# A graph network on one core: POOL's rests moved between chunk gathers and node gathers

## The reference

```python
# layer L0 (src, dst of all edges)
h = einsum('ni,hio->nho', x, W_att)
alpha = segment_softmax(leaky_relu(h[src] @ a_src + h[dst] @ a_dst), dst)
local = segment_sum(alpha * h[src], dst).mean(heads)
glob = x
for _ in range(2):                                   # two hops
    glob = segment_sum(glob[src], dst) / deg
x = x + concat(local, glob @ W_g + b_g) @ W_w + b_w
# layers L1, five times
h = leaky(x @ W1 + b1) @ W2 + b2
e = leaky(edge_attr @ We1 + be1) @ We2 + be2
out = x + segment_sum(h[src] * e * dot_scale, dst) * res_w
x = layernorm(out) * ln_g + ln_b
```

## Time and profile before

| | us |
|---|---|
| median of 3 runs | 6910.15 |
| lowest, highest | 6908.07, 6911.17 |
| the profiled execution | 6893.8 |
| its span, first to last instruction | 6892.0 |
| POOL busy in the span | 5142.3 (75%) |
| DVE busy | 5197.8 (75%) |
| PE busy | 5232.0 (76%) |

### The profile page before, as it was taken

How to read it: one execution, slowest core, us unless ns; L and a number is a source line. 1 busy time by engine, 2 the same in 40 slices (tenths; PEclk the granted TensorE clock), 3 DMA queues, 4 the chain that set the end, 5 groups by cost and what they waited for, 6 DMA issues and landing times.

```text
span 6892.0 us, 140780 instructions
## 1 busy us (share of the span) xinstructions
PE 5232.0 (76%) x51990; PEld 4800.9 (70%) x51995; DVE 5197.8 (75%) x12225; ACT 4110.2 (60%) x6886; POOL 5142.3 (75%) x7040
## 2 busy tenths in 40 slices
PE   7888843333333489998799997999979999799997
PEld 6878732222222388888788887888878888788887
DVE  7877666666666578888688886888878888688887
ACT  4666626555555356666466664666646666466664
POOL 6777777777777467776677775777757777577776
PEclk9999965656555689999899997999979999799998
DMA  4444426777777433333233332333323333233332
GB/s 108 109 106 113 107 69 229 240 245 238 240 236 241 139 85 100 99 97 97 66 97 101 98 98 68 98 99 97 98 67 98 99 96 97 68 96 98 97 99 76
DMA packets 505340, 828.89 MB, mean 120 GB/s; under 512 B 110911, under 2 KB 218038, under 8 KB 491599
## 3 DMA queue, kind: packets, MB, share of 16 engines
q1 hardware_dynamic: 373374, 655.05, 28.3%
q0 software_dynamic: 131280, 164.84, 13.4%
HBM read 385.06 MB, written 434.48 MB: 119 GB/s over the span
## 4 chain that ended last, share of the span: by engine, by line
PE 52%; issue 7%; DVE 4%; ACT 1%; another core or an unknown queue 1%; POOL 1%; DMA 0%; POOLq 0%; DVEq 0%; ACTq 0%
PE psum L1372 45%; PE psum L1386 6%; DVE arena L1773 1%; POOL agg L719 1%; DVE by_lane L1836 0%; ACT gring L1010 0%; PE psum L1298 0%; DVE psum L1819 0%; PE psum L1329 0%; ACT gring L1014 0%; DVE xin L1773 0%; ACT run L995 0%; DVE arena L1790 0%; DMA agg<-rowsg,last_i 0%
## 5 line engine op out<-in xcount | busy, mean ns | idle before, releaser
L712 POOL DMA_INDIRECT gring<-tableh,src_i x2525 | 2480.6, 982 | 863.0 <-issue 587.9
L1372 PE MATMUL psum<-penalty,arena 125*128 125x192 bf16 x25755 | 2474.9, 247 | 248.3 <-issue 227.7
L1372 PEld LDWEIGHTS psum<-penalty,arena 125*128 125x128 bf16 x25755 | 2154.3, 98 | 365.0 <-issue 336.4
L1773 DVE TENSOR_SCALAR arena<-dst_f,node_id 125x768 bf16<-125x768 f16 x4301 | 1762.4, 457 | 0.1
L712 POOL DMA_INDIRECT gring<-table,src_i x1364 | 1384.3, 1015 | 441.2 <-issue 317.1
L703 POOL MEMSET diag<- 128x256 f32 x2916 | 1061.1, 364 | 228.8 <-DMA tableh<-arena 116.7
L985 ACT COPY psum<-diag 128x512 f32<-128x512 f32 x505 | 297.5, 590 | 1338.4 <-issue 765.9
L1813 DVE TENSOR_REDUCE gring<-psum 128x192 f32<-128x576 f32 x505 | 381.9, 756 | 765.9 <-remote 421.2
L1149 PE MATMUL psum<-ident,by_lane 128*128 128x128 f32 x202 | 66.2, 431 | 882.2 <-DMA by_lane<-attr_last 754.6
L1149 PEld LDWEIGHTS psum<-ident,by_lane 128*128 128x128 f32 x202 | 29.1, 203 | 941.1 <-issue 941.1
L923 ACT ACTIVATE arena<-gring,es_w 128x65 f32<-128x65 f32 x1616 | 398.3, 335 | 456.4 <-DMA gring<-table,src_i 445.0
(11 more groups left out here) (280 smaller groups left out, 8748.0 us busy)
## 6 DMA issues: line engine op xcount, KB each, us to landing
rows<-arena SPq DMA_DIRECT2D x101, 1296.0 KB
acts<-arena SPq DMA_DIRECT2D x505, 256.0 KB
arena<-acts SPq DMA_DIRECT2D x505, 256.0 KB
rowsg<-run SPq DMA_DIRECT2D x505, 256.0 KB
dst_f<-pe_src SPq DMA_DIRECT2D x557, 93.8 KB
gring<-tableh,src_i POOLq DMA_INDIRECT x2525
rows<-run SPq DMA_DIRECT2D x101, 256.0 KB
gring<-table,src_i POOLq DMA_INDIRECT x1364
```

What stands on the lines that cost most here:

```text
L712: pool.indirect_dma_start(ring[:, s, k, :], None, table, bass.IndirectOffsetOnAxis(ap=src_i[:, c * K + k:c * K + k + 1], axis=0))\
L1372: ins = mm(found(n)[:, m, :], hot_at(n // 2, j)[:, at:at + P], parts[:, j, :, :].rearrange("q a f -> q (a f)"), start=(j == 0), stop=(j == ...
L1773: ins = ts(hot_at(pair, j), src_row[b], node_id[:, j:j + 1], None, ALU.is_equal)
```

## The change

The counting moves into a helper `paced(burst)`: before a gather, if `burst` gathers were issued since the last rest or reset, it rests and begins to count again. `gather_chunk` gets a parameter `burst` (4 unless given) and `gather_nodes` calls `paced()` before each of its 25 gathers, having set the count to zero. The count is also set to zero ahead of the second pass and ahead of each layer. The second pass calls `gather_chunk` with a burst of K = 8.

```diff
+            def paced(burst=BURST):
+
+                if issued[0] == burst:
+                    pause()
+                    issued[0] = 0
+                issued[0] += 1
+
-            def gather_chunk(c, s, table, ring, ready, cols):
+            def gather_chunk(c, s, table, ring, ready, cols, burst=BURST):
                 for k in range(cols):
-                    if issued[0] and issued[0] % BURST == 0:
-                        pause()
-                    issued[0] += 1
+                    paced(burst)
                     pool.indirect_dma_start(ring[:, s, k, :], None, table,
                                             bass.IndirectOffsetOnAxis(ap=src_i[:, c * K + k:c * K + k + 1], axis=0))\
                         .then_inc(ready[s], 16)
 
             def gather_nodes(rows, to, arrived):
 
+                issued[0] = 0
                 for j in range(NJ):
+                    paced()
                     pool.indirect_dma_start(to[:, j, :], None, rows,
                                             bass.IndirectOffsetOnAxis(ap=last_i[:, j:j + 1], axis=0))\
                         .then_inc(arrived[j // GJ], 16)
...
             pool.wait_ge(t2_out, NG * 16)
             settle()
+            issued[0] = 0
             for c in range(CH):
                 if c >= SL:
                     pool.wait_ge(hopcopy, c - SL + 1)
                     pool.wait_ge(msg_steps, (c - SL + 1) * (K - ON_ACT))
                     settle()
-                gather_chunk(c, c % SL, table2, gather2, g2_ready, K)
+                gather_chunk(c, c % SL, table2, gather2, g2_ready, K, K)
...
                 pool.wait_ge(table_out, (l + 1) * (NG * 16))
                 settle()
+                issued[0] = 0
                 for c in range(CH):
```

## The result

| | before | changed |
|---|---|---|
| median | 6909.11 us (6908.05 to 6911.17, 4 runs) | 6797.38 us (6788.06 to 6801.15, 4 runs) |
| profiled execution | 6893.8 us, span 6892.0 | 6788.06 us, span 6786.2 |
| ratio, 95% interval | | 0.9836, 0.9819 to 0.9853 |

What follows compares the result with a forecast made beforehand. PE was taken to bound the layers, POOL's instruction stream the second pass. Removed rests -103.5, contention +6, added rests +18, resets -1 gave -80 us: 6830 us against the median of 6910.15, range 6806 to 6860 us.

Steps and rivals of the forecast that it cites:

- The second pass: Paced by POOL's instruction stream; 102 rests removed give -103.5 us, with the contention term -97.5 us.
- The contention term: Second pass: with shorter chunks more of DVE's work meets gathers and stretches them, giving back 6 us.
- the one of transfers that give half back: Second pass: gathers queue behind row stores and POOL waits for buffers; 6875 us, chance 0.12.
- the one of stretching gathers: Second pass: gathers without a rest between them stretch to 1.43 us; about 7150 us, slower, chance 0.04.
- DVE's waits for gathers near 1.6 us a chunk: Second pass: sign that the forecast is right, from a mean wait of 2.6 us before.
- Cost of the added rests: Node gathers: 3 us after the first pass, 1 after the second, 8 in layers 0 to 3, 6.2 in layer 4.
- ACT's 8.39 us: Layers 0 to 3, behind the second node group: idle time that may hide the rests' delay; 2 us a layer taken.
- rival 1: Node gathers: all 42 added rests lie on the path, 43 us in place of 18; 6855 us, chance 0.08.
- Cover, not path: Layers' chunk gathers: PE bounds there and POOL's gathers run ahead, so the rests kept there cost no time.

Runs made afterwards that it cites:

- the part alone: Changed kernel without rests in the node gathers, the second pass still resting once per chunk: 6798.31 us, 0.9866 of the kernel before.
- A: Kind of run set in which the kernel before took 6892 to 6909 us (medians of three sets, the main comparison among them).
- -16 us alone: Changed kernel with the second pass resting at every fourth gather again, node rests kept: 6878.5 us, 0.9977 of the kernel before.
- the grid: Changed kernel in one set: three memsets per rest, with/without node rests, 6802.66/6811.96 us; one memset, 8070.03/8082.77 us.
- B: Kind of run set in which the kernel before took 6740 to 6748 us (three sets).

## Why the prediction was right, and where it failed

- **The second pass: right.** -97.5 us forecast, -92.4 in the profiled pair and -93 by the part alone; POOL waits 1.4 us for others, gathers take 1.034 us, the DMA share is 0.78. The contention term held. Of the rivals, the one of transfers that give half back, and the one of stretching gathers, are out. The rule of the Trainium skill (SBUF — State Buffer, § Who interferes with whom) that a DVE instruction with two SBUF inputs doesn't contend with a GpSimd instruction that only writes agrees with the second pass again: the rests' memsets take 317 and 318 ns beside VectorE's work. In the layers they do take longer, 380 ns in the mean of 2500 to 3200 us before; there it is 438 ns beside VectorE's L1773 and 317 where VectorE idles.
- **What that part lost was not foreseen.** The sign "DVE's waits for gathers near 1.6 us a chunk" failed: they came to 0.4, because VectorE waited for ACT, and ACT for PE, which stands still beside runs of eight gathers on A. It cost little there because POOL was still later; without rests it turned the gain round.
- **The node rests: the step that failed.** "Cost of the added rests: 3 + 1 + 8 + 6.2 = 18 us." On A they measured -16 us alone and -9 in the grid. Term by term, in the profiled pair: first +5.8 for 3, behind the second pass -17.5 for +1, between the layers -22.2 for +8, last +11.2 for +6.2. The two outer groups cost more than forecast (in the last layer the six rests alone lengthen the gathers from 31.6 to 39.5 us) and the five inner ones gained. Not all of the -22.2 is the rests' doing: from the first node gather to the next layer's first gather it is 60 us in place of 63 in each of the four gaps, 12 us in all, as in the grid (13 us), and the other 10 lie ahead of the node gathers, where executions differ. The 41 us by which these stages miss the forecast, 31 without those 10, are more than the whole miss of the profiled pair, 26 us: 5 us less in the second pass, 5 in the first pass and 5 in the layers stand against them.
- **Its exact place** is the sentence on ACT's 8.39 us: "if that doesn't move with DVE, it hides the delay". I took the idle time as something that could hide a cost. On A it was a loss that the rests make smaller. The row that should have been asked for stands a few lines above it in the same timeline of before:

```profile
3287.41 1.61 PE L1318 MATMUL psum<-xT,arena 64*128 64x125 f32 x10 [0.70 <-ACT xT L961]
```

  PE's result was there by 3289.02 by its row and ACT came for it at 3298.39, all beside an unbroken run of gathers. I asked what the rests cost, and never what the run without them cost. What holds PE's work or its signal up there stays open.
- **On B the same step has the right sign and is too small:** 37 us. That is near rival 1 (all 42 rests on the path, 43 us), though those behind the second pass cost nothing (119.9 and 120.3 us from its last gather to layer 0's first). ACT's 8.39 us of idle time are A's alone: on B ACT L975 starts 0.9 us behind PE L1325's end.
- **"Cover, not path" for the layers' rests: wrong.** Two facts of the trace stood side by side, PE's 45% of the chain and POOL's 2525 gathers with little but "issue" before them; I read the first. The sum did not rest on it, but a reader would have left the largest gain (B) or the largest danger (A) alone.
- **The range** bounded the node rests at 8 to 35 us. Nothing in the rows excluded a gain, so the lower bound had no reason; a bound of -16 us would have held the result, by 2 us.

## What to carry to other kernels

A pause that a tuned kernel makes on purpose is first asked what runs badly without it: look at the other engines' unexplained stops beside a long unbroken run of the engine that pauses, then price the pause. Don't change such a constant on the word of one set of runs: here one memset instead of three is 0.893 in one kind and 1.170 in the other, and what makes the kind isn't known. The changed kernel is faster than before on both kinds (0.984 to 0.986 and 0.988), and so is the one without rests in the first and last node gathers, which was as good on A and 13 us better on B; it is the one that I would take.

## What the runs showed of the hardware that I had not expected

- The same kernel can run in two ways that differ in how long PE stands still beside POOL's indirect gathers. With one memset to a rest, PE's weight loads of L1381 stood still without a named cause for 1010 us on A and had no such wait on B; the times were 8070 and 6021 us. Whether the chip makes the difference isn't shown.
- On A it matters how long a run of gathers is and how long the rest before it: at three memsets a rest, PE's pauses are nearly absent beside a run's first two gathers and frequent from the third on; at one memset they are there beside all four.
- PE's stops cost twice: with one memset on A, the granted clock was at its lower level for 1025 of the 4907 us of the layers' chunk gathers, where it was 65 of 4042 us with three memsets.
- A rest costs POOL more than its memsets: in the second pass with three memsets the next gather starts 1.33 us after the last one's end, in a layer with one memset 0.60, without any 0.30. With one memset, a second rest to a chunk cost 0.6 us in the second pass.
- What holds PE up on A was not found: neither the packets of the instruction queue nor the layers' gathers are slower there (in the second pass of the changed kernel a gather takes 1.05 us on A and 1.02 on B). Whether another break in POOL's stream than a memset would do, or fewer and larger gathers, was not tried.
